# Linear attention and a spiking feed-forward block on one core: phase two's sync queue reordered, and four small moves in the other queues

## The reference, cut to what matters

```python
x = x + attn(layernorm(x))              # linear attention, 16 heads of 64
#   q, k = elu(xn@Wq)+1, elu(xn@Wk)+1;  v = xn@Wv
#   z = q . k.sum(rows) + 1e-6;  kv = k^T v  per head
#   out = ((q @ kv) / z) @ Wo + bo
x = x + ffn(layernorm(x))
#   h = relu(xn @ W_fc^T)^2;  y = h @ W_proj^T
#   mem = 0; five times: reset = mem > 1; mem = 0.9*mem + y - reset; spk = mem > 1
#   ffn = sum(spk) / 5
```

## Time and profile before

| | us |
|---|---|
| median of 3 runs (lowest, highest) | 1049.34 (1048.62, 1049.93) |
| the profiled execution | 1048.78 |
| its span | 1047.0 |
| PE busy | 1030.8 (98%) |
| DVE busy | 936.9 (89%) |
| ACT busy | 704.7 (67%) |
| POOL busy | 637.9 (61%) |

### The profile page before, as it was taken

One profiled execution on the slowest core, in us unless ns is written; L12 is line 12 of the kernel. 1 busy time (PEld: TensorE's weight loads), 2 busy tenths in 40 slices (PEclk: granted clock), 3 DMA queues, 4 the chain that ended last, 5 costly groups with the idle time before them and its releaser, 6 DMA issues.

```text
span 1047.0 us, 20427 instructions
## 1 busy us (share of the span) xinstructions
PE 1030.8 (98%) x7364; PEld 691.8 (66%) x7364; DVE 936.9 (89%) x1871; ACT 704.7 (67%) x1145; POOL 637.9 (61%) x404
## 2 busy tenths in 40 slices
PE   8999999999999999999999999999999999999997
PEld 4444444444444467677777778787878787878886
DVE  7799888898888798999999999999999999999966
ACT  6788677777768748566666667575757575757643
POOL 1444344455345477767777776768676777676833
PEclk9999999999999999999999999999999999999999
DMA  5545544325323543345444554365435443554341
GB/s 140 135 127 145 114 119 90 79 62 121 86 76 83 125 79 84 76 101 119 104 102 106 106 102 91 87 111 119 90 86 119 111 90 86 120 112 79 76 77 46
DMA packets 265141, 104.27 MB, mean 100 GB/s; under 512 B 219344, under 2 KB 262480, under 8 KB 265040
## 3 DMA queue, kind: packets, MB, share of 16 engines
q1 hardware_dynamic: 265040, 102.97, 43.8%
HBM read 33.69 MB, written 16.79 MB: 48 GB/s over the span
## 4 chain that ended last, share of the span: by engine, by line
PE 86%; DVE 9%; DMA 2%; issue 2%; ACT 1%; SPq 0%; POOL 0%; ACTq 0%; DVEq 0%
PE proj L565 29%; PE acc L593 15%; PE acc L679 13%; PE acc L695 13%; PE acc L721 13%; DVE spikes L1162 2%; DVE feat L1080 1%; DVE xnat L1001 1%; DVE feat L1006 1%; DVE zsum L1084 1%; DMA qT<-feat 1%; PE proj L615 1%; PE acc L651 1%; PE proj L627 1%; DVE spikes L1159 1%
## 5 line engine op out<-in xcount | busy, mean ns | idle before, releaser
L771 ACT ACTIVATE feat<-proj 128x1024 f32<-128x1024 f32 x124 | 126.8, 1023 | 213.8 <-PE proj L565 213.7
L1291 POOL TENSOR_TENSOR qT<-qT,feat 128x1024 f32<-128x1024 f32 x60 | 142.3, 2371 | 175.3 <-DVE xnat L1001 151.7
L1326 POOL TENSOR_TENSOR h<-h_f,h 128x512 f16<-128x512 f32 x128 | 152.1, 1208 | 93.7 <-ACT h L899 93.7
L721 PE MATMUL acc<-wpT,h 128*128 128x256 f16 x1536 | 178.0, 273 | 1.9 <-DVE spikes L1162 1.9
L565 PE MATMUL proj<-wk,xT 128*128 128x512 f16 x768 | 176.1, 379 | 2.6 <-DMA xT<-xnat 2.4
L695 PE MATMUL acc<-xn2T,wfcT 128*128 128x256 f16 x1536 | 178.0, 273 | 0.0
L679 PE MATMUL acc<-m_all,qT 128*128 128x256 f16 x1488 | 174.1, 274 | 3.1 <-DMA qT<-feat 3.1
L593 PE MATMUL acc<-feat,xnat 128*128 128x512 f16 x768 | 176.2, 379 | 0.0
L695 PEld LDWEIGHTS acc<-xn2T,wfcT 128*128 128x128 f16 x1536 | 150.3, 98 | 28.9
L1006 DVE SCALAR_TENSOR_TENSOR feat<-proj,feat 128x1024 f32<-128x1024 f32 x124 | 150.3, 1212 | 20.1 <-ACT feat L775 19.4
L565 PE MATMUL proj<-wq,xT 128*128 128x512 f16 x720 | 165.2, 379 | 0.0
(11 more groups left out here) (81 smaller groups left out, 1172.1 us busy)
## 6 DMA issues: line engine op xcount, KB each, us to landing
x_t<-in_L_attn_x_dram SPq DMA_DIRECT2D x128, 128.0 KB, 2.3
xT_spill<-xT SPq DMA_DIRECT2D x64, 128.0 KB, 2.1
out_dram<-out_t SPq DMA_DIRECT2D x64, 128.0 KB, 2.1
xT<-xT_spill SPq DMA_DIRECT2D x60, 128.0 KB, 2.3
ks_all<-ks_rows SPq DMA_DIRECT2D x4, 512.0 KB, 4.6
qT<-feat SPq DMA_TRANSPOSE x120, 3.2
m_all<-in_L_attn_Wk_dram SPq DMA_DIRECT2D x4, 256.0 KB, 3.9
xT<-xnat SPq DMA_TRANSPOSE x64, 2.4
```

The costliest lines, as they stand in the source:

```text
L721: mm = pe.matmul(y_at(n), h[:, pair % 2, left, f, u * P:(u + 1) * P], wpT[:, right, f::FB, :], start=(i == 1), stop=(i == FB * len(PRODUCTS)))
L771: act.activation(dst, proj[:, place, :], ACT.Relu, scale=-1.0 / QK_SCALE).then_inc(neg, 1)
L1291: pool.tensor_tensor(kacc[:, b % 2, :], kacc[:, b % 2, :], k_feat(n), ALU.add).then_inc(k_added, 1)
L1326: pool.tensor_tensor(lo, h_f[:, k % 4, :], hi, ALU.subtract).then_inc(h_lo, 1)
```

## The change

Five moves; no instruction is added, removed or altered.

- SP in a step: x's load, the load of q's operand, q's two turns, xn's turns, the store. Before: xn's turns, the load of q's operand, x's load, the store, q's turns.
- ACT at step 64: q(63)'s high half ahead of the relu and the halves of f1(57).
- POOL at step 64: q(63)'s low half right behind its normalisation, ahead of h's low halves; before, it was first in step 65.
- DVE from step 63 on: the comparisons and the writing ahead of xn's low halves and of q's five instructions (so far in step 10 alone).
- DVE at steps 25 and 28: the low part of the last M behind q's instructions and the comparisons; before, it was behind the second of q's instructions.

```diff
@@ sync
             for t in STEPS:
+                if live(t):
+                    load_x_b(t)
+                if live(t + 4):
+                    load_xT(t + 4)
+                if t > FILLED and live(t - 2):
+                    turn_q_both(t - 2)
                 for n in at(o_step, t - 2):
                     if n % 2:
                         turn_xn2(n - 1)
                         turn_xn2(n)
-                if live(t + 4):
-                    load_xT(t + 4)
-                if live(t):
-                    load_x_b(t)
                 for n in at(f2_step, t - 2):
                     store_out(n)
-                if t > FILLED and live(t - 2):
-                    turn_q_both(t - 2)
@@ scalar
+                if t == TILES:
+                    q_hi_tile(t - 1)
                 for n in at(f1_step, t):
                     if n >= 4:
                         relu_of(n)
                         h_hi_of(n)
-                if live(t - 1):
+                if t < TILES:
                     q_hi_tile(t - 1)
@@ vector
                 spiking = at(f2_step, t - 1)
-                if t == FILLED + 1:
-                    for k in range(5):
-                        spike_step(0, k)
-                    write_out(0)
+                spikes_first = t == FILLED + 1 or t >= TILES - 1
+                if spikes_first:
+                    for n in spiking:
+                        for k in range(5):
+                            spike_step(n, k)
+                        write_out(n)
...
-                    if k == 1 and t + 1 in LATE:
-                        m_lo_job(*LATE[t + 1][1:])
-                    if t > FILLED + 1:
+                    if not spikes_first:
                         for n in spiking:
                             spike_step(n, k)
-                if t > FILLED + 1:
+                if t + 1 in LATE:
+                    m_lo_job(*LATE[t + 1][1:])
+                if not spikes_first:
                     for n in spiking:
                         write_out(n)
@@ gpsimd
-                if t > FILLED and live(t - 2):
+                if FILLED < t <= TILES:
                     q_lo_tile(t - 2)
                 if t > FILLED and live(t - 1):
                     normalise_q(t - 1)
+                if t == TILES:
+                    q_lo_tile(t - 1)
```

## The result

The changed kernel takes 1053.61 us (median of 6, 1053.04 to 1054.29), the one before 1049.32 (6 runs beside it): ratio 1.0042, 95% interval 1.0032 to 1.0053. It is slower by about 4.4 us by that ratio (4.3 between the medians). The forecast was 1052.4, slower with 0.64. The profiled execution after took 1054.29, the slowest of its six, around a span of 1052.5, which is 5.5 more than the span before; 0.5 of that comes before the changed part of the program (the first block of phase two, o(0), starts at 377.97, before at 377.51).

A forecast was written before the change was run, and what follows sets the result against it. PE was taken to bound the kernel, so the change could only give back or add PE stalls. Terms +0.3 - 0.3 - 0.8 + 2.3 + 1.6 = +3.1 us, forecast 1052.4 us, 8-in-10 range 1048.6 to 1055.2.

The forecast's parts named there:

- Part 1, SP's order: Steps 10 to 12: o(8)'s wait goes but lay in DVE's shadow; f2(3) taken as +0.3 us, bounds -1.7 to +1.2.
- The walk: Following DVE and POOL through steps 10 to 12 by instruction: f2(3) between 0.8 us late and as before.
- rival C: Even steps: POOL's bias goes ahead of waiting L1080, 26 steps at 0.4 make +11, 1063 us; chance 0.03.
- the term of -0.3 to 0 for the even steps: Steady even steps: earlier bias lets zeps take 0.16 instead of 0.42; gain 0.3 us at most, taken as 0.3.
- The 3.8 us: Step 11 in the profile before: PE idle while o(8) waits 1.98 us, its low clock and a little late f2(3).
- Part 2, M's low part: Steps 25 and 28: f2(19) no longer waits for its comparisons; -0.8 us, bounds -0.8 and 0.
- Part 3, the drain: Steps 63 on: DVE's comparisons first delay residual(60), o(61) and xn's turns; +2.3 us at o(62), +1.6 at f1(62).
- o(62): Drain, output product of tile 62: from 1001.92 to between 1003.1 and 1005.3, +1.2 to +3.4 us, taken as +2.3.
- rival D: New waits at f2(2) and o(61) drop PE to 1.2 GHz, about 1.7 us each; uncovered once 1054.1 us; chance 0.10.
- Part 4, nothing: Step 64, ACT and POOL: q(63)'s halves moved ahead of f1's cost nothing and gain nothing.
- Rivals A and B: A: drain stalls mostly go, 1046.9 us, chance 0.12. B: cheaper steps 10 to 12 offset the drain, centre 1050, chance 0.22.

The follow-up runs named there:

- thin_sp: Kernel before with SP's new order alone, plus part of POOL's work left out in steps 10 to 13: 1045.72 us, ratio 0.9969.
- halves_alone: Kernel before with only ACT's and POOL's moves of q(63)'s halves: 1048.38 us, ratio 0.9997.
- drain_undone: Changed kernel with DVE's drain order put back as before the change: 1046.26 us, ratio 0.9974.
- sp_and_m_low: Kernel before with only SP's new order and M's late low part behind the comparisons: 1047.26 us, ratio 0.9980.
- drain_alone: Kernel before with only DVE's comparisons first from step 63 on: 1058.24 us, ratio 1.0088.
- lo_first: Changed kernel with xn's low parts again ahead of the comparisons from step 64 on, step 63 left as changed: 1049.14 us, ratio 0.9999.
- light_before: Kernel before with four comparisons of tiles 1 and 2 cut to 8 of 256 columns: 1048.26 us, ratio 0.9993.
- m_low_alone: Kernel before with only M's late low part moved behind the comparisons: 1048.04 us, ratio 0.9992.

## Why the prediction was right

**Part 1, SP's order: right.** o(8) is on time, f2(2) waits 1.92 for the comparisons, and f2(3) is 0.08 earlier from o(0) where I took 0.3 later. That the wait was hidden is shown by the table: f2(3) is at 74.2 to 74.6 in all eleven kernels with untouched work in that stretch, whether o(8) waits or not. thin_sp shows the cover. The walk itself held in its steps: bias got between the two low parts, L1082 waited for q_lo(9) at 430.00 and no longer at 436.12. The rival C, POOL ahead of a waiting L1082 in every even step, did not come: f2(3) to f1(55) has no new stall. In even steps I had looked at one place, though. In step 28 SP's order alone cost 1.0 where a tenth decided whether zeps ran ahead of h_lo: the term of -0.3 to 0 for the even steps had no such case. In the change part 2 covered it. The 3.8 us that the prediction counts as PE's stall at o(8) hold for the one profile of before: in four others with the same wait the clock's 1.7 is absent, and in the three of them with untouched work f2(3) is at most 0.4 earlier.

**Part 2, M's low part: right in sign, -0.8 forecast.** The gain at f2(19) is 0.83 beyond f2(3)'s 0.08 in the change; with small waits of later even steps gone too, f1(55) is 1.26 earlier. That answers to the -0.8 and -0.3 of the sum.

**Part 3, the drain: the mechanism right, one size short.** DVE was idle 1.52 before spikes(53), as worked out. residual(60): forecast 993.0 to 994.2 in the time of before; it came at 992.97 with f1(55) 0.81 earlier, so 993.8. o(61) +2.66 (forecast +1.7 to +3.0), f2(55) +1.74 (+1.2 to +2.3), f1(58) +4.07 (landing of the turn +2.5 to +4.6), f1(62) a further 1.91 (1.6). The term that was mis-sized is o(62): +4.41 where I took +2.3 and bounded it at 3.4. 1.66 of it is the low clock: f1(58) takes 4.28 from start to start in place of 2.62. I had it as rival D with 0.10 and as covered at o(61); it came one block later, behind f1(58)'s wait, where nothing covers it. The other 0.45 is that the landing fell in the upper half. In size the result (1053.61) is nearer to rival D's 1054.1 than to the forecast's 1052.4, though D placed its low clock elsewhere.

**Part 4, nothing: right with DVE's old drain** (halves_alone; drain_undone against sp_and_m_low). Under the new one the rows of drain_alone say that it spared some 2.5 us, which the prediction did not have; it had the moves in its walk, so the sum did not suffer.

The sum was +3.1; measured is +4.4 (3.4 to 5.6). Part of that closeness is luck: the sum was worked out for one execution, and there the blocks from o(0) to f1(62) came 5.06 later, 2.0 over the sum; the median of six lies lower than the one that was profiled. Whether the clock fell in the other five is not shown. Rivals A and B needed residual(60) before 991.2 or a cheaper transition; neither came.

## What to carry to other kernels

A wait on the chain of what ended last is worth its length only if nothing else is due behind it: in every kernel here whose work was whole, f2(3) came at 74.2 to 74.6 with or without o(8)'s wait. Before removing one, look at the next two places where the same engine meets the busy one. Placing the urgent work first on an in-order engine costs twice, by the idle time until its input is there and by what stood behind it (here the turns of xn, with 2.4 us of transfer still to come). Two engines that hold each other up are one resource (zeps of 0.16 us took 1.84 behind q_lo(62)); where a tenth decides who goes first, an edit elsewhere moves it by 1 us.

## What the runs showed of the hardware that I had not expected

The length of PE's wait does not alone say whether its clock falls. Behind o(61)'s wait, 2.99 by its row and of the same length in all three, it fell in drain_alone (0.66 over 994 to 999) and not in lo_first (window below) or in the change. Behind o(8)'s wait it fell in the profile of before (1.98) and not in light_before (1.97, second row and window below), nor in m_low_alone, whose wait was longer (2.3 at most by its waits). A low stretch cost 1.5 to 1.7 us each time. The first window is lo_first's.

```profile
992.00:997.00 5.00, 3.54 (x31) 2.97 (x32) 4.74 (x14) 4.73 (x9) 2.71 (x2) 1.00 0.28 56
...
437.94 2.79 PE L679 MATMUL acc<-m_all,qT 128*128 128x256 f16 x24 [1.97 <-DMA qT<-feat]
...
438.00:443.00 5.00, 5.00 (x47) 4.47 (x48) 4.96 (x17) 2.90 (x5) 5.00 (x5) 1.00 0.61 134
```

The start of phase two itself moved between 377.3 and 379.3 over these executions, though nothing ahead of it differs, which is as much as most parts of the change are worth.
